# Ends of two softmax attention layers in a four-layer transformer kernel: channel order made by DMA during the layer, and results taken chunk by chunk

## The chip, the cores and the metric

The kernel runs on one core of one Trainium2 chip. The time is the device time of one execution in microseconds (us). The core has TensorE (PE; its weight loads are listed as PEld), VectorE (DVE), ScalarE (ACT), GpSimd (POOL), SyncE (SP), and 16 DMA engines. SP computes nothing here and issues most DMAs. Each engine runs its own instructions in order and waits for others on semaphores.

## The reference, cut to what matters

x has 2 batches of 1024 tokens of 128 channels in float32. Four layers follow one another, each an attention and a feed-forward part, each with a modulated layernorm in front and a gated residual. The change concerns the ends of the attention in layers 0 and 1:

```
# layer 0: two softmax maps per head, 16 heads of 8 channels
lam  = exp(sum(lambda_q1*lambda_k1)) - exp(sum(lambda_q2*lambda_k2)) + LAMBDA_INIT
attn = (map0 - lam * map1) @ v
attn = attn * rsqrt(mean(attn^2 over the 8 channels of a head) + 1e-5)
attn = attn * subln_w * (1 - LAMBDA_INIT)
x    = x + ga * (attn @ Wo.T)
# layer 1: plain softmax attention with a key mask, 16 heads
x    = x + ga * (softmax(q k^T / sqrt(8)) v @ Wo.T + bo)
# then, in both layers, layernorm of x and the feed-forward part
```

## The kernel before, in words

x stays in SBUF as [128 channels, 2, 1024]. NC = 4 chunks c of CW = 512 tokens cut it: chunk 0 and 1 are batch 0, chunk 2 and 3 batch 1. PSUM is one tensor `ps` of 8 banks of 512 columns.

**The softmax stage** (`softmax_stage`, used by layer 0 with the tile prefix a0 and by layer 1 with a1) works in units u, 32 in layer 0 and 16 in layer 1. Two groups of four maps make a pair kk (PAIRS is 8 and 4), and a pair has two halves of 512 queries, so n = 2*kk + half counts 16 halves in layer 0 and 8 in layer 1, with two units per half. In a unit PE makes scores in eight slots of keys (line 833), ACT takes their exponential (919), PE multiplies with the values (847) into bank 6, and meanwhile DVE finds the row maxima of the next unit (products 813, reduction 938), which POOL splits into bf16 parts (765 to 773). In the last unit there is no next one.

When a half is complete, ACT copies bank 6 to `o` (`take`, 899). Rows 32*j + 16*g + 0..7 of `o` hold 8 channels of map j of group g, row +8 its denominator. For every half but the last, SP then moves the denominators through DRAM into a packed tile (729, 731), ACT takes Ln and Exp there (904, 909; at slot 5 of the unit after the `take`), SP brings the reciprocals back through DRAM, broadcast over the rows (733, 735), and POOL divides (`divide`, 778) into `A.on`, which holds all halves. For the odd halves up to n = 11 SP then issues 36 loads of operands for later pairs (415), for the even ones from n = 2 to n = 12 it issues 12. SP takes up the next half only after them. The last half has no unit to hide behind: `take`, a product that spreads the denominators (`spread`, 856), Ln and Exp on ACT (929, 931), and a division on DVE (`divide_last`, 960).

**The end of layer 0** (`diff_out_stage`, line 1014) begins when all 16 halves are divided. Per chunk four products with `pick` (1031) accumulate map0 - lam*map1 in channel order; ACT squares (1059), DVE copies out scaled by the sub-norm weight (1068); `head_sum` (1036) adds the squares of a head, ACT takes Ln and Exp (1061, 1063), `head_spread` (1041) spreads the result over the channels, DVE multiplies (1072), PE multiplies with Wo (1044), DVE adds to x (1076). Each step runs over all four chunks before the next begins.

**The end of layer 1** (`out_stage` with the name o1 and two parts, line 1083) waits for all 8 halves, makes two products per chunk (1094), and DVE adds the bias (1123) and then the gated sum (1126).

Both ends interleave on PE the products of the following norm: `centre(c)` (302, bank 4 + c) once x of the chunk is there, `variance(c)` (307, bank c). The norm's ACT program squares (328), and takes Ln and Exp (332, 334), in the order square 0, square 1, invert 0, square 2, invert 1, square 3, invert 2, invert 3; DVE applies (314, 316). The norm's SP program (321) loads the weights of the next part; on SP it stands right behind the softmax stage's. A float32 product of 512 columns is two matmul instructions in the trace.

Of the kernel before, what the change touches and what calls it, by code (L numbers as in the profile page):

```python
# [15 lines left out]
F32 = mybir.dt.float32  # L16
# [619 lines left out]
def softmax_stage(nc, R, ctx, W, A):  # L636
# [26 lines left out]
    logged, inverted, divided, last_rec = (sem(n) for n in ("logged", "inverted", "divided", "last_rec"))  # L663
    den_dram, rec_dram = (nc.dram_tensor(pre + n, [2, 8, CW], F32, kind="Internal").ap() for n in ("den", "rec"))
# [49 lines left out]
    def on_sp(sp):  # L714
# [11 lines left out]
        for n in range(2 * PAIRS - 1):  # L726
# [14 lines left out]
            if n >= 2 and not c and kk - 1 < PAIRS:  # L741
                for operand in range(2):
                    load_rows(A, 2 * kk - 1, (kk - 1) % 2 * 2 + 1, operand, sp, heads=range(2, 4))

    def on_pool(pool):
# [38 lines left out]
        for u in range(UNITS - 1):  # L784
# [6 lines left out]
            if u and u % 2 == 0:  # L791
                divide(u // 2 - 1)

    def on_pe(pe):
# [94 lines left out]
        for half in range(2):  # L889
            pv(UNITS - 1, 7, half)  # L890
        spread()

    def on_act(act):
# [32 lines left out]
        take(PAIRS - 1, 1)  # L926
        act.wait_ge(bank_full, filled("spread"))
        act.wait_ge(divided, 2 * PAIRS - 2)
        act.activation(rec[:, 1, :], R.ps[:, dve_bank("spread"), :], ACT.Ln).then_inc(last_rec, 1)
        act.wait_ge(last_rec, 1)  # L930
        act.activation(rec[:, 1, :], rec[:, 1, :], ACT.Exp, scale=-1.0).then_inc(last_rec, 1)

    def on_dve(dve):
# [22 lines left out]
        def divide_last():  # L956

            dve.wait_ge(last_rec, 2)
            dve.wait_ge(divided, 2 * PAIRS - 1)
            dve.tensor_tensor(A.on[:, PAIRS - 1, CW:T], o[:, 1, :], rec[:, 1, :], ALU.mult).then_inc(divided, 1)  # L960
# [20 lines left out]
        divide_last()  # L981
# [32 lines left out]
def diff_out_stage(nc, R, ctx, W, A, join):  # L1014

    PAIRS = A.groups // 2 // B
# [3 lines left out]
    a, sq = R.xc, R.sq  # L1020
    dev = sb("dev", [128, 2, CW])
    got, copied, squared, ms, deviated, inverted, spread, normed, proj, done = (
        sem(n) for n in ("got", "copied", "squared", "ms", "dev", "inverted", "spread", "normed", "proj", "done"))
    A.finished, join.ready = (done, NC), [(done, c + 1) for c in range(NC)]

    def on_pe(pe):
        pe.wait_ge(*A.divided)
        for c in range(NC):
            b, t = chunk(c)
            for g in range(PAIRS):  # L1030
                last = pe.matmul(R.ps[:, c, :], pick[:, g, :], A.on[:, b * PAIRS + g, t], start=(g == 0),
                                 stop=(g == PAIRS - 1))
            last.then_inc(got, 1)
        for c in range(NC):
            pe.wait_ge(squared, c + 1)
            last = pe.matmul(R.ps[32 * c:32 * c + 32, 4, :], W.head_sum[:], sq[:, c, :], start=True, stop=True)
        last.then_inc(ms, 1)
        pe.wait_ge(inverted, 1)
        pe.wait_ge(copied, NC)
        for c in range(NC):  # L1040
            pe.matmul(R.ps[:, c, :], W.head_spread[:, c, :], dev[:, 1, :], start=True, stop=True).then_inc(spread, 1)
        for c in range(NC):
            pe.wait_ge(normed, c + 1)
            pe.matmul(R.ps[:, 4 + c, :], wo[:], a[:, c, :], start=True, stop=True).then_inc(proj, 1)
            if c == 2:
                join.norm.centre(pe, 0)
        join.norm.centre(pe, 1)
        join.norm.variance(pe, 0)
        join.norm.centre(pe, 2)
# [6 lines left out]
    def on_act(act):  # L1056
        for c in range(NC):
            act.wait_ge(got, c + 1)
            act.activation(sq[:, c, :], R.ps[:, c, :], ACT.Square, scale=8 ** -0.5).then_inc(squared, 1)
        act.wait_ge(ms, 1)  # L1060
        act.activation(dev[:, 0, :], R.ps[:, 4, :], ACT.Ln, bias=R.eps[:]).then_inc(deviated, 1)
        act.wait_ge(deviated, 1)
        act.activation(dev[:, 1, :], dev[:, 0, :], ACT.Exp, scale=-0.5).then_inc(inverted, 1)

    def on_dve(dve):
        for c in range(NC):
            dve.wait_ge(squared, c + 1)
            dve.tensor_scalar(a[:, c, :], R.ps[:, c, :], cols[:, 7:8], None, ALU.mult).then_inc(copied, 1)
        for c in range(NC):
            dve.wait_ge(copied, c + 1)  # L1070
            dve.wait_ge(spread, c + 1)
            dve.tensor_tensor(a[:, c, :], a[:, c, :], R.ps[:, c, :], ALU.mult).then_inc(normed, 1)
        for c in range(NC):
# [3 lines left out]
                                     ALU.mult, ALU.add).then_inc(done, 1)  # L1077
        join.norm.apply(dve, 0)
# [4 lines left out]
def out_stage(nc, R, ctx, W, layer, half, name, rhs, parts, w, ready, join, bias=None):  # L1083

    tmp = R.rstd
    proj, biased, done = (nc.alloc_semaphore(name + n) for n in ("proj", "biased", "done"))
    join.ready = [(done, c + 1) for c in range(NC)]

    def on_pe(pe):
        pe.wait_ge(W.loaded, W.count)  # L1090
        for c in range(NC):
            pe.wait_ge(*ready(c))
            for i in range(parts):
                last = pe.matmul(R.ps[:, c, :], w[:, i, :], rhs(i, c), start=(i == 0), stop=(i == parts - 1))  # L1094
                if parts > 2 and c == 3 and i == parts // 2:
# [3 lines left out]
            if c == 2 or c == 3 and parts <= 2:  # L1099
# [1344 lines left out]
```

## Time and profile before

| | us |
|---|---|
| median of 3 runs | 2280.16 |
| lowest and highest of them | 2278.03, 2281.89 |
| the profiled execution | 2285.85 |
| its span in the trace | 2284.1 |

The execution that was profiled took 2285.85 us; all rows are from it. Times in the trace count from the start of its span, and 1.75 us of the execution lie outside the span. The mean granted clock of TensorE over the span was 0.974 of full speed. The softmax stage of layer 0 ends near 684 us, that of layer 1 near 1124 us. Layers 2 and 3 follow and aren't touched but for two waits.

### The profile page before, as it was taken

The numbers are of one execution on the slowest core, as the hardware profiler recorded it, in microseconds if no ns is written. First come the engines' busy times: TensorE is split into PE (matmuls) and PEld (weight loads), VectorE is DVE, ScalarE is ACT, GpSimd is POOL, SyncE is SP. The second block draws the span as 40 slices with busy tenths as digits, with TensorE's granted clock in tenths as the row PEclk, the third lists the DMA queues.
The fourth block names the chain that finished last, engine by engine and source line by source line (L and its number), as shares of the span: only waits on it lengthen the run. The fifth ranks groups of instructions, "written<-read, shape, count | busy, mean of one in ns | idle before, by whom it ended". The sixth has DMA issues, their size and how long they took to land. (4 is left out here: it accounts for less than half of the span.)

```text
span 2284.1 us, 40826 instructions
## 1 busy us (share of the span) xinstructions
PE 2092.2 (92%) x15948; PEld 926.4 (41%) x15948; DVE 1597.6 (70%) x2012; ACT 1359.4 (60%) x2700; POOL 212.8 (9%) x393
## 2 busy tenths in 40 slices
PE   5899999999989689999989999999998989999999
PEld 3222222222224222222336666656666434444454
DVE  5999999999954699999365555555555265555553
ACT  3599999999983369999744444444444232222243
POOL 3011111010102501111000000000000010000000
PEclk7799999999999789999999999999999999999999
DMA  4000000000000200110100100011010125455520
GB/s 134 15 13 20 24 20 17 19 25 19 16 23 0 86 28 17 30 37 10 28 4 11 23 14 16 18 17 20 11 20 17 29 49 129 114 127 117 123 63 19
DMA packets 107966, 86.76 MB, mean 38 GB/s; under 512 B 50837, under 2 KB 91669, under 8 KB 103824
## 3 DMA queue, kind: packets, MB, share of 16 engines
q1 hardware_dynamic: 105780, 82.77, 14.7%
q8 instruction: 122, 2.00, 0.4%
q10 hardware_dynamic: 668, 1.04, 0.1%
q0 software_dynamic: 1344, 0.52, 0.1%
q14 instruction: 52, 0.43, 0.1%
HBM read 75.63 MB, written 8.73 MB: 37 GB/s over the span
## 5 line engine op out<-in xcount | busy, mean ns | idle before, releaser
L919 ACT ACTIVATE a0p<-ps 128x512 f32<-128x512 f32 x1024 | 544.3, 599 | 88.4 <-PE ps L833 71.8
L938 DVE TENSOR_REDUCE a0nm<-ps 128x2 f32<-128x1024 f32 x512 | 586.1, 1212 | 13.1 <-PE ps L813 10.9
L847 PE MATMUL ps<-a0p,a0vst 128*32 128x256 f32 x4096 | 328.6, 393 | 28.1 <-ACT a0p L919 14.6
L919 ACT ACTIVATE a1p<-ps 128x512 f32<-128x512 f32 x512 | 275.6, 596 | 57.2 <-PE ps L833 48.2
L938 DVE TENSOR_REDUCE a1nm<-ps 128x2 f32<-128x1024 f32 x256 | 294.2, 1213 | 11.5 <-PE ps L813 10.6
L833 PE MATMUL ps<-a0qm,a0k 32*128 32x512 bf16 x1024 | 276.8, 387 | 0.0
L1674 DVE TENSOR_REDUCE canm<-ps 128x1 f32<-128x128 f32 (+7 forms) x256 | 182.0, 752 | 115.3 <-PE ps L1537 114.6
L1625 ACT ACTIVATE cap_long<-ps,canm 128x1024 f32<-128x1024 f32 (+3 forms) x128 | 121.6, 953 | 190.1 <-DVE canm L1674 190.1
L813 PE MATMUL ps<-a0k,a0q 32*128 32x512 bf16 x1024 | 203.8, 396 | 29.4 <-DVE a0nm L938 21.7
L1906 ACT ACTIVATE ex_s<-ps 128x512 f32<-128x512 f32 x128 | 76.4, 597 | 252.9 <-PE ps L1861 252.9
L813 PE MATMUL ps<-a1k,a1q 64*128 64x512 bf16 x512 | 150.2, 404 | 27.0 <-DMA a1k<-a1mask 14.9
L847 PE MATMUL ps<-a1p,a1vst 128*32 128x256 f32 x2048 | 163.9, 392 | 7.0 <-ACT a1p L919 6.1
L1995 DVE TENSOR_TENSOR ex_su<-ex_s,ps 128x512 f32<-128x512 f32 x128 | 88.1, 688 | 116.9 <-PE ps L1865 115.7
L833 PEld LDWEIGHTS ps<-a0qm,a0k 32*128 32x128 bf16 x1024 | 79.1, 91 | 209.1 <-ACT a0p L919 119.8
L1537 PE MATMUL ps<-cak,caq 64*128 64x512 f32 (+3 forms) x768 | 158.6, 517 | 0.0
L833 PE MATMUL ps<-a1qm,a1k 64*128 64x512 bf16 x512 | 156.2, 385 | 0.0
L1550 PE MATMUL ps<-ident_res,cap_long 128*128 128x128 f32 x832 | 123.2, 281 | 29.1 <-ACT cap_long L1625 18.8
L847 PEld LDWEIGHTS ps<-a0p,a0vst 128*32 128x32 f32 x4096 | 81.5, 108 | 156.3 <-ACT a0p L919 71.0
L1865 PE MATMUL ps<-h_res,f2wu 128*128 128x512 f32 x256 | 130.7, 592 | 0.0
L1861 PE MATMUL ps<-h_res,f2wg 128*128 128x512 f32 x256 | 130.7, 592 | 0.0
L1849 PE MATMUL ps<-ex_hid,f2wd 128*128 128x512 f32 x256 | 130.5, 592 | 0.0
L1550 PEld LDWEIGHTS ps<-ident_res,cap_long 128*128 128x128 f32 x832 | 89.0, 140 | 86.0 <-issue 39.2
(300 smaller groups left out, 2535.5 us busy)
## 6 DMA issues: line engine op xcount, KB each, us to landing
ex_wb<-ex_w_dram SPq DMA_DIRECT2D x62, 512.0 KB, 6.2
carrow<-car_dram SPq DMA_DIRECT2D x32, 256.0 KB, 4.3
xc_res<-a0rec SPq DMA_DIRECT2D x15, 256.0 KB
a0parts<-a0parts_sb SPq DMA_DIRECT2D x8, 384.0 KB, 3.6
a1parts<-a1parts_sb SPq DMA_DIRECT2D x8, 384.0 KB, 3.5
f2wg<-in_ex_gate SPq DMA_DIRECT2D x32, 64.0 KB, 1.8
f2wu<-in_ex_up SPq DMA_DIRECT2D x32, 64.0 KB, 1.9
f2wd<-in_ex_down SPq DMA_DIRECT2D x32, 64.0 KB, 1.9
```

The lines of the kernel that those rows point to most:

```text
L813: pe.matmul(R.ps[:, bank + d, :], q[rows, slot, rt, t0:t0 + 128], k[rows, slot, rt, hf * CW:(hf + 1) * CW], start=True, stop=True).then_in ...
L833: pe.matmul(R.ps[:, score_bank(n), :], k[rows, place(u)[3], rt, s * 128:(s + 1) * 128], qm[rows, u % 2, rt, :], start=True, stop=True).the ...
L847: last = pe.matmul(R.ps[32 * j:32 * j + 32, 6, cols], vst[:, g, s, j * HG // 4, :], p[:, s % 2, j, cols], start=(g == 0 and s == 0 and hal ...
L919: act.activation(p[:, s % 2, e, :], R.ps[:, score_bank(n), :], ACT.Exp).then_inc(exp_done, 1)
L938: dve.tensor_reduce(nm[:, u % 2, tb, 2 - 2 * z:4 - 2 * z, hf], R.ps[:, bank:bank + 2, :], X_AXIS, ALU.max, negate=True).then_inc(bank_free, 1)
L1537: last = pe.matmul(R.ps[:, 2 * hh + c, 0:cols], q[rows, hp % 2, b, tb * 128:(tb + 1) * 128], k[rows, hp % 2, b, c * CW:c * CW + cols], sta ...
L1550: last = pe.transpose(R.ps[:, bank, to:to + 128], p[long][:, hh, s * 128:(s + 1) * 128], R.ident[:])
L1625: act.activation(p[long][:, hh, 0:(tb + 1) * 128], src, ACT.Exp, bias=nm[:, a % 4:a % 4 + 1], accum_out=rs[:, b, tb, hh:hh + 1]).then_inc( ...
L1674: dve.tensor_reduce(nm[:, a % 4:a % 4 + 1], src, X_AXIS, ALU.max, negate=True).then_inc(max_done, 1)
L1849: pe.matmul(R.ps[:, i % 4, :], wd[:, (i // 4) % 2, :], hid[:, i % 4, :], start=False, stop=True, skip_group_check=True).then_inc(d_done, 1)
L1861: pe.matmul(R.ps[:, G_BANK + 2 * (i % 2), :], wg[:, slot, :], h_chunk(R, c), start=True, stop=True)\
L1865: pe.matmul(R.ps[:, U_BANK + 2 * (i % 2), :], wu[:, slot, :], h_chunk(R, c), start=True, stop=True)\
```

## The change

In layer 0:

- After each of the first 15 halves is divided, SP issues eight DMAs of 8 rows by 512 columns. They move the rows of `A.on` into `A.maps`, in channel order, one tile for map 0 and one for map 1. `A.on` now holds two halves in turn. SP waits for the division first, and these DMAs stand on SP behind the operand loads of that half. POOL waits, before it divides half n, for the DMAs of half n - 2.
- At the end of its softmax program, DVE forms map0 - lam*map1 by one instruction per chunk (128 rows, for chunk 3 the 96 rows that don't come from the last half), into `rstd`, in the order 0, 1, 3, 2. POOL squares each.
- On PE three `head_sum` products (chunks 0 to 2) stand ahead of the last two value products of the last unit (`last_products`); on ACT their Ln and Exp stand ahead of the last `take`. `head_spread` for chunk 0 stands ahead of the `spread` product, those of chunks 1 and 2 and the Wo product of chunk 0 behind it. Between these DVE does the sub-norm multiply (one instruction for weight and norm), the last division, and the addition to x.
- The last half passes one `pick` product with 32 output rows, then square, `head_sum`, Ln, Exp and `head_spread` for chunk 3 on 32 rows.

In layer 1 `value_out_stage` takes the place of `out_stage`: the product of chunk 0 stands ahead of `last_products`, that of chunk 1 behind `spread`, that of chunk 2 waits for 7 halves, that of chunk 3 for 8. The bias times the gate is added to x by DVE before the first result. Cut to its core:

```diff
@@ on_sp, for each half n but the last, behind the operand loads
+            if A.maps:
+                b, pair = n // 2 // (PAIRS // B), n // 2 % (PAIRS // B)
+                sp.wait_ge(divided, n + 1)
+                for g in range(2):
+                    for j in range(4):
+                        r, ch = 32 * j + 16 * g, 32 * pair + 16 * g + 8 * (j // 2)
+                        sp.dma_start(A.maps[ch:ch + 8, j % 2, b, c * CW:c * CW + CW], A.on[r:r + 8, c, :]).then_inc(gathered[c], 16)
@@ on_pool
         def divide(n):
             pool.wait_ge(rec_in[n % 2], 16 * (n // 2 + 1))
+            if A.maps and n >= 2:
+                pool.wait_ge(gathered[n % 2], 128 * (n // 2))
...
+        if A.maps:
+            for i, (c, rows) in enumerate(COMBINED):
+                pool.wait_ge(combined, i + 1)
+                pool.tensor_tensor(R.sq[rows, c, :], R.rstd[rows, c, :], R.rstd[rows, c, :], ALU.mult).then_inc(map_squared, 1)
@@ on_dve of the softmax stage
-        divide_last()
+        if A.maps:
+            for c, rows in COMBINED:
+                b, t = chunk(c)
+                halves = (b + 1) * (PAIRS // B) - (c == 3)
+                dve.wait_ge(gathered[c % 2], 128 * halves)
+                dve.scalar_tensor_tensor(R.rstd[rows, c, :], A.maps[rows, 1, b, t], W.cols[rows, 4:5], A.maps[rows, 0, b, t],
+                                         ALU.mult, ALU.add).then_inc(combined, 1)
@@ diff_out_stage, on_pe
-        pe.wait_ge(*A.divided)
-        for c in range(NC):
-            b, t = chunk(c)
-            for g in range(PAIRS):
-                last = pe.matmul(R.ps[:, c, :], pick[:, g, :], A.on[:, b * PAIRS + g, t], start=(g == 0),
...
+        pe.wait_ge(A.map_squared, 4)
+        for c in range(3):
+            last = pe.matmul(R.ps[32 * c:32 * c + 32, MS[0], :], W.head_sum[:], sq[:, c, :], start=True, stop=True)
+        last.then_inc(ms, 1)
+        A.last_products()
+        pe.wait_ge(inverted, 1)
+        head_spread(0)
+        A.last_spread()
+        head_spread(1)
+        head_spread(2)
+        output(0)
+        pe.wait_ge(*A.divided)
+        pe.matmul(R.ps[late, PICKED, :], pick[:, 3, late], A.on[:, 1, :], start=True, stop=True).then_inc(picked, 1)
+        output(1)
+        pe.wait_ge(squared, 1)
+        pe.matmul(R.ps[late, MS[1], :], W.head_sum[:], sq[:, 3, :], start=True, stop=True).then_inc(ms, 1)
+        output(2)
+        join.norm.centre(pe, 0)
+        pe.wait_ge(copied, 1)
+        pe.wait_ge(inverted, 2)
+        head_spread(3)
         join.norm.centre(pe, 1)
         join.norm.variance(pe, 0)
+        output(3)
@@ diff_out_stage, on_act
+        invert(0, early)
+        A.last_take()
+        A.last_reciprocal()
+        act.wait_ge(picked, 1)
+        act.activation(sq[late, 3, :], R.ps[late, PICKED, :], ACT.Square).then_inc(squared, 1)
+        invert(1, late)
@@ diff_out_stage, on_dve
+        norm(0)
+        norm(1)
+        A.last_divide()
+        norm(2)
+        result(0)
+        dve.wait_ge(squared, 1)
+        dve.tensor_copy(a[late, 3, :], R.ps[late, PICKED, :]).then_inc(copied, 1)
+        result(1)
+        result(2)
+        dve.wait_ge(copied, 1)
+        norm(3)
+        result(3)
         join.norm.apply(dve, 0)
@@ value_out_stage (new, layer 1), on_pe
+        output(0)
+        A.last_products()
+        A.last_spread()
+        output(1)
+        output(2)
+        join.norm.centre(pe, 0)
+        output(3)
+        join.norm.variance(pe, 0)
+        join.norm.centre(pe, 1)
+        join.norm.centre(pe, 2)
+        join.norm.variance(pe, 1)
+        join.norm.centre(pe, 3)
+        join.norm.variance(pe, 2)
+        join.norm.variance(pe, 3)
@@ value_out_stage, on_dve
+        dve.tensor_scalar(lift[:], R.gate[:, 2 * B:3 * B], W.bo[:], None, ALU.mult).then_inc(lifted, 1)
+        dve.wait_ge(lifted, 1)
+        for b in range(B):
+            dve.tensor_scalar(R.x[:, b], R.x[:, b], lift[:, b:b + 1], None, ALU.add).then_inc(lifted, 1)
+        result(0)
+        A.last_divide()
+        for c in range(1, NC):
+            result(c)
+        join.norm.apply(dve, 0)
```

## Rows read from the trace of the kernel before

**Rows 1.** The page: busy us of each engine (share of the span), instructions.
```profile
PE 2092.2 (92%) x15948; PEld 926.4 (41%) x15948; DVE 1597.6 (70%) x2012; ACT 1359.4 (60%) x2700; POOL 212.8 (9%) x393
```

**Rows 2.** Timeline, end of layer 0: start us, us, engine, line, out<-in, count [idle before <-releaser].
```profile
679.28 1.07 PE L847 MATMUL ps<-a0p,a0vst 128*32 128x256 f32 x16 [0.60 <-ACT a0p L919]
680.42 0.60 ACT L899 ACTIVATE a0o<-ps 128x512 f32<-128x512 f32 x1 [1.19 <-PE ps L847]
682.25 0.60 ACT L929 ACTIVATE xc_res<-ps 128x512 f32<-128x512 f32 x1 [1.23 <-PE ps L856]
683.54 0.69 DVE L960 TENSOR_TENSOR a0on<-a0o,xc_res 128x512 f32<-128x512 f32 x1 [23.38 <-ACT xc_res L931]
684.29 15.68 PE L1031 MATMUL ps<-a0on,a0pick 128*128 128x512 f32 x32 [2.08 <-DVE a0on L960]
701.74 0.69 ACT L1061 ACTIVATE do_dev<-ps,eps_res 128x512 f32<-128x512 f32 x1 [1.14 <-PE ps L1036]
706.67 2.74 PE L1044 MATMUL ps<-xc_res,a0wo 128*128 128x512 f32 x6
711.17 0.75 DVE L1076 SCALAR_TENSOR_TENSOR x_res<-ps,gate_res,x_res 128x512 f32<-128x512 f32 x1 [0.96 <-PE ps L1044]
714.40 1.02 PE L302 MATMUL ps<-x_res,centre_res 128*128 128x512 f32 x2
714.62 0.68 ACT L332 ACTIVATE rstd_res<-ps,eps_res 128x512 f32<-128x512 f32 x1
```

**Rows 3.** Windows (busy us of each engine, clock, DMA share, GB/s) at the ends.
```profile
683.00:684.00 1.00, 0.00 (x0) 0.00 (x0) 0.46 (x1) 0.51 (x1) 0.00 (x0) 1.00 0.00 0
685.00:686.00 1.00, 1.00 (x2) 0.34 (x1) 0.00 (x0) 0.00 (x0) 0.00 (x0) 0.50 0.00 0
688.00:689.00 1.00, 1.00 (x3) 0.38 (x2) 0.00 (x0) 0.00 (x0) 0.00 (x0) 1.00 0.00 0
1145.00:1150.00 5.00, 3.23 (x6) 0.78 (x6) 4.78 (x9) 2.00 (x4) 0.00 (x0) 1.00 0.01 3
```

**Rows 4.** Timeline of POOL and SP late in layer 0, the same columns.
```profile
662.70 1.27 POOL L778 TENSOR_TENSOR a0on<-a0o,xc_res 128x512 f32<-128x512 f32 x1 [4.74 <-DMA xc_res<-a0rec]
646.42 0.58 SPq L729 DMA_DIRECT2D a0den<-a0o  x1
648.19 0.32 SPq L731 DMA_DIRECT2D a0packed<-a0den  x1
659.89 1.31 SPq L321 DMA_DIRECT2D f0w<-in_L_fW2T  x1
666.96 0.43 SPq L321 DMA_DIRECT2D decay_res<-in_L_norm  x1
```

**Rows 5.** Timeline of SP and ACT around the tightest and an ordinary odd half.
```profile
264.07 3.67 SPq L415 DMA_DIRECT2D a0k<-a0parts  x6
268.23 0.62 SPq L729 DMA_DIRECT2D a0den<-a0o  x1
277.67 0.24 ACT L904 ACTIVATE a0packed<-a0packed 128x32 f32<-128x32 f32 x1
413.29 3.67 SPq L415 DMA_DIRECT2D a0k<-a0parts  x6
428.94 0.24 ACT L904 ACTIVATE a0packed<-a0packed 128x32 f32<-128x32 f32 x1
```

**Rows 6.** Timeline, end of layer 1, and the bias of layer 0's feed-forward part.
```profile
733.85 3.10 DVE L1267 TENSOR_SCALAR x_res<-x_res,ff0lift 128x1024 f32<-128x1024 f32 x2
1120.57 0.60 ACT L899 ACTIVATE a1o<-ps 128x512 f32<-128x512 f32 x1 [1.19 <-PE ps L847]
1124.53 7.08 PE L1094 MATMUL ps<-a1on,a1wo 128*128 128x512 f32 x12 [2.17 <-DVE a1on L960]
1135.08 0.60 ACT L328 ACTIVATE sq_res<-ps 128x512 f32<-128x512 f32 x1 [1.98 <-PE ps L302]
1137.32 0.69 DVE L314 TENSOR_TENSOR xc_res<-rstd_res,ps 128x512 f32<-128x512 f32 x1 [1.56 <-ACT rstd_res L334]
```

More of the change, by code:

```diff
@@ L888, in on_pe, with last_products @@
                     turn(u + 1)
-        for half in range(2):
-            pv(UNITS - 1, 7, half)
-        spread()
+        def last_products():
+            for half in range(2):
+                pv(UNITS - 1, 7, half)
+        A.last_products, A.last_spread = last_products, spread
     def on_act(act):
@@ L925, in on_act, with last_reciprocal @@
                         invert(u // 2 - 1)
[L926 to L931, printed above, removed]
+        def last_reciprocal():
+            act.wait_ge(bank_full, filled("spread"))
+            act.wait_ge(divided, 2 * PAIRS - 2)
+            act.activation(rec[:, 1, :], R.ps[:, dve_bank("spread"), :], ACT.Ln).then_inc(last_rec, 1)
+            act.wait_ge(last_rec, 1)
+            act.activation(rec[:, 1, :], rec[:, 1, :], ACT.Exp, scale=-1.0).then_inc(last_rec, 1)
+        A.last_take, A.last_reciprocal = lambda: take(PAIRS - 1, 1), last_reciprocal
     def on_dve(dve):
@@ L1034, in on_pe, with head_spread @@
[L1034 to L1042, printed above, removed]
+        def head_spread(c):
+            rows = late if c == 3 else early
+            pe.matmul(R.ps[:, SPREAD[c], :], W.head_spread[rows, c, :], dev[rows, 1, :], start=True, stop=True).then_inc(spread, 1)
@@ L1056, in on_act, with invert, norm, result @@
     def on_act(act):
[L1057 to L1063, printed above, removed]
-    def on_dve(dve):
[L1066 to L1070, printed above, removed]
+        def invert(i, rows):
+            act.wait_ge(ms, i + 1)
+            act.activation(dev[rows, 0, :], R.ps[rows, MS[i], :], ACT.Ln, bias=R.eps[rows], scale=0.125).then_inc(deviated, 1)
+            act.wait_ge(deviated, i + 1)
+            act.activation(dev[rows, 1, :], dev[rows, 0, :], ACT.Exp, scale=-0.5).then_inc(inverted, 1)
+        invert(0, early)
[4 more added lines that the diff above has]
+        invert(1, late)
+    def on_dve(dve):
+        def norm(c):
             dve.wait_ge(spread, c + 1)
-            dve.tensor_tensor(a[:, c, :], a[:, c, :], R.ps[:, c, :], ALU.mult).then_inc(normed, 1)
-        for c in range(NC):
+            dve.scalar_tensor_tensor(a[:, c, :], a[:, c, :], cols[:, 7:8], R.ps[:, SPREAD[c], :], ALU.mult, ALU.mult)\
+               .then_inc(normed, 1)
+        def result(c):
             b, t = chunk(c)
@@ L1087, in out_stage @@
+def out_stage(nc, R, ctx, W, layer, half, name, rhs, parts, w, ready, join):
+    proj, done = (nc.alloc_semaphore(name + n) for n in ("proj", "done"))
     join.ready = [(done, c + 1) for c in range(NC)]
@@ L1098, in on_pe @@
             last.then_inc(proj, 1)
-            if c == 2 or c == 3 and parts <= 2:
-                join.norm.centre(pe, c - 2)
-            if c == 3 and parts <= 2:
-                join.norm.variance(pe, 0)
-        if parts <= 2:
-            join.norm.centre(pe, 2)
-            join.norm.variance(pe, 1)
-            join.norm.centre(pe, 3)
-        else:
-            join.norm.variance(pe, 1)
-            join.norm.centre(pe, 2)
-            join.norm.centre(pe, 3)
+            if c == 2:
+                join.norm.centre(pe, 0)
+        join.norm.variance(pe, 1)
+        join.norm.centre(pe, 2)
+        join.norm.centre(pe, 3)
         join.norm.variance(pe, 2)
@@ L1115, in on_dve @@
     def on_dve(dve):
-        dve.wait_ge(W.loaded, W.count)
         for c in range(NC):
```

77 lines of the change are left out of this document (49 added, 28 removed).

## The prediction

> **What bounds the kernel now.** I read the page first: PE is busy for 92% of the span [rows 1], but a busy share doesn't say what a stage's end costs, so I went to the timeline of the two ends. In layer 0 the last exponentials are followed by a chain in which each engine waits for another: value products, `take`, spread, Ln, Exp, division, and only then, at 684.29, the 32 `pick` instructions, 15.68 us long [rows 2]. The windows show that PE, which had only the `spread` product between 680.4 and 684.3, then works at half clock (0.50, that is 1.2 GHz) and is back at full (2.4 GHz) by 688 [rows 3]. After `pick` comes the second chain, Ln, Exp, `head_spread`, multiply, Wo, to the last addition at 711.17 and `centre(3)` at 714.40 [rows 2]. Only half 15 needs the first chain: half 14 was divided at 662.70, and neither DVE nor POOL has other work afterwards [rows 4]; DVE's 23.38 us of idle time before line 960 say the same [rows 2]. Layer 1 ends likewise, with 7.08 us for the first 12 product instructions [rows 6]. So the bound is latency on one chain, not an engine, and what is taken off that chain comes off the time.
>
> **Prices.** A float32 product of 512 columns costs PE 0.86 us: six instructions of Wo took 2.74, one lasts 0.59, so the pitch is (2.74 - 0.59)/5 = 0.43 and a product has two. From issue to its reader's start it is 1.23 - 0.1 = about 1.1 us [rows 2]. On ACT Copy or Square costs 0.60, Ln 0.69, Exp 0.63, on DVE 0.69 to 0.75, on POOL 1.27 [rows 2, 4].
>
> **Layer 0, covered work.** Half 14 is divided at 664.0. SP then issues eight DMAs. The trace has no SBUF to SBUF copy; its nearest row is the store of the denominators, also 8 rows of 2 KB: 0.58 to 0.62 to issue, and the next DMA, which waits for it, starts 1.77 after it [rows 4, 5]. Bounds: 0.32 (the packed load) to 1.31 (the largest load) each [rows 4]; I take 0.6. Eight end at 668.8 and the last lands near 670. DVE combines (0.75), POOL squares (1.27): 672.2. The squares of chunks 0, 1 and 3 (3 x 1.27 from 664.0) are done at 667.8. PE needs all four at about 678.6, so 6 us are spare; the cover is the last unit, and without it the chain of 8 us would be paid in full. The weight loads of the next part (line 321), which began right after the broadcast of half 14 and ended by 667.4 [rows 4], move back by up to 9 us, to 677; the feed-forward part uses them after 690.
>
> **Layer 0, mid-stage.** The eight DMAs also stand behind the 36 operand loads of the six odd halves up to 11. Ordinarily those end at 413.29 + 3.67 = 416.96, and ACT takes the Ln of the next half at 428.94; in the tightest case they end at 267.74 and Ln starts at 277.67 [rows 5]. The store of the denominators, the packed load and its landing take about 1.8 + 2.0 = 3.8 us (the 2.0 is an estimate from the 1.77 of the same-sized store). That leaves 8.2 and 6.1 us for eight issues, 1.02 and 0.77 us each; at 0.6 nothing stalls (zero cost, cover 1.3 us in the worst half). POOL's new wait for the DMAs of half n - 2 and the queue of loads for later pairs have tens of us.
>
> **Layer 0, the new tail**, with PE at full clock. PE is free at 678.6, three `head_sum` deliver at 679.7. ACT: Ln, Exp to 681.1, then `take` to 681.7 (0.7 later than before: the price of putting them ahead of it). `head_spread(0)` fills PE to 682.0, `spread` reaches ACT at 683.1, Ln and Exp end at 684.4. Meanwhile `head_spread` 1 and 2 and Wo(0) run to 685.4. DVE divides after its second multiply, to 685.4; `pick` reaches ACT at 686.6, Square (687.2), `head_sum` (688.4), Ln and Exp (689.7). PE fills in with Wo(1), Wo(2) and `centre(0)`. Then four products in PE's order, `head_spread(3)`, `centre(1)`, `variance(0)`, Wo(3), end at 693.2; DVE's last addition starts at 693.4; `centre(2)`, `variance(1)` follow and `centre(3)` starts at 694.9 instead of 714.40. The norm's second Ln starts at 695.0 instead of 714.62 [rows 2]. Gain **19.5 us**.
>
> **Layer 1.** Wo(0), two products or 1.72 us, starts when PE is free at 1118.7 and delays the last value products: `take` starts 1.0 later than 1120.57. `spread` leaves PE at 1123.1, chunks 1 and 2 take until 1126.5 while ACT and DVE finish the last half (1125.4), `centre(0)` to 1127.4, chunk 3 to 1129.1, `variance(0)`, and `centre(1)` to 1130.8. ACT's Square of chunk 1 starts at 1131.0 instead of 1135.08, and from there ACT works without gaps; the first apply on DVE starts at 1133.0 instead of 1137.32 [rows 6]. The bias additions (3.10 us on DVE, by the two in layer 0 [rows 6]) lie in its idle last unit. Gain **4.3 us**. Bounds for this term: 3 (apply pushed behind the results on DVE) to 6 (the start of `variance(0)` moves by 5.8).
>
> **Sum.** 19.5 + 4.3 = 23.8 us, so 2285.85 - 23.8 = 2262.0 for the profiled execution. That one took 5.7 us more than the median; the median of the runs comes to 2280.16 - 23.8 = **2256.4**.
>
> **A rule that speaks against it.** The store of 16 KB took 0.6 us to issue and 1.77 to complete, and six loads are issued in 3.67 us without waiting for one another [rows 4, 5]. The Trainium skill, page DMA: Bandwidth & Descriptors, section Rules for kernel authors, says that transfers under 64 KB pay mostly overhead and should be joined; its section Latency and other measured facts names about 2 us of fixed cost. If eight DMAs paid that one after another, an estimate by that page would be 16 us a half. By the rows the overhead overlaps; the rule's outcome is the second rival, priced from rows there.
>
> **Rival 1: the clock falls in the new tails.** Before, it fell after 4 us in which PE was nearly idle and came back after 3.5 us of full work; at 65% busy (3.23 of 5.00) it stayed at 2.4 GHz [rows 3]. In the new tails I count PE busy for over 80% between 681 and 688 and for about 70% between 1121 and 1124.5, which speaks for a full clock. Against: many short waits. At half clock a product costs 0.86 more. On the path stand twelve in layer 0 (some 8 uncovered, 7 us) and ten in layer 1 (some 6, 5 us): 2256.4 + 12 = **2268.4**. The skill's page TensorE: Matmul & The Clock Gate, section HAM oscillation — how this bites in real kernels, tells of short bursts of products between waits that each begin cold; it would choose this rival. Chance 0.15.
>
> **Rival 2: slower, through SP's queue.** SP is in order, and behind the eight DMAs waits the next half's store of denominators, for which ACT stalls amid the exponentials of slot 5; PE and everything else wait for ACT. With d us for each DMA, five halves lose 8d - 8.2 and one 8d - 6.1. At d = 1.31 that is 5 x 2.3 + 4.4 = 16, and the gain shrinks to 8. It decides from 48d - 47.1 = 23.8, d = 1.48. At d = 2 (each issued only when the one before is done, as 1.77 suggests [rows 4]), the loss is 49 us; moreover the last half lands at about 681 and PE waits some 5 us: 2256.4 + 49 + 5 = **2310**. For it: the one completion that the trace shows. Against: 36 loads in a row at 0.61 each [rows 5]. Chance 0.04.
>
> **Rival 3: part of it is lost to stalls.** DMAs at 1.0 to 1.31, or POOL and DVE late, so that PE waits at 678.6, or the feed-forward weights late: **2266**. Chance 0.06.
>
> **Rival 4: more comes back.** The full clock keeps a second stretch alive in the norm or the feed-forward part, and layer 1 gives 6: **2252**. Chance 0.07. That the change doesn't do what it says is hard to see, since all its instructions are plain in the diff; a cost I haven't seen that takes back the gain within 0.2% or beyond: 0.03.
>
> **How the numbers follow.** The forecast has 0.65. The range reaches from Rival 4, less 1 us of scatter between runs, to Rival 1 with the same: 2251 to 2269.5. It holds the forecast, Rival 4, most of Rival 1 and of Rival 3. Left out are Rival 2, the unseen cost and the outer parts of the others. A measurement of this kernel can tell about 0.2%, 4.6 us, from no change. Faster by more: the forecast, Rivals 1, 3 and 4, 0.93; within it 0.03; slower 0.04, Rival 2 and a little of the unseen.
>
> **What would show each step.** Line 1031's 32 instructions are gone, and two with 32 output rows stand after the last division. The gather DMAs last about 0.6 us on SP, the last eight end near 669, and the Ln of each later half starts in ACT's rhythm, 37.8 us after the one before, without a gap. POOL's four squares end before 673 and PE doesn't wait between the last scores and `head_sum`. `take` starts near 681.1 and 1121.6, the granted clock stays 1.00 from 681 to 696 and from 1121 to 1134, and `centre(3)` starts near 695 in layer 0. A clock of 0.50 in either tail speaks for Rival 1, gaps before ACT's Ln in slot 5 for Rival 2. The prediction is wrong if the span between the last exponential and the norm's first apply shrinks by less than 15 us in layer 0, or if the attention stage itself gets longer.

## The result, and the profile after

The change took the median from 2280.26 us (4 runs) to **2264.11 us** (4 runs, 2262.16 to 2265.14), a ratio of 0.9929 [0.9912, 0.9946]: 16.1 us gained where 23.8 were forecast. The profiled execution took 2265.14 us, the longest of the four. The page after, to be held against [rows 1]:

```profile
span 2263.4 us, 40899 instructions
PE 2077.2 (92%) x15918; PEld 918.9 (41%) x15918; DVE 1595.7 (71%) x2012; ACT 1358.9 (60%) x2699; POOL 216.5 (10%) x397
```

PE's busy time fell by 15.0 us, about what `pick` took (15.68 us [rows 2]); its share is what it was. The new end of layer 0 in the timeline of after, beside [rows 2] (columns: start, length, engine, line, operation, tiles, shape, count, and the idle time before it with its releaser):

```profile
676.26 1.03 PE L1078 MATMUL ps<-sq_res,a0head_sum 128*32 128x512 f32 x6
677.35 0.68 ACT L1110 ACTIVATE do_dev<-ps,eps_res 96x512 f32<-96x512 f32 x1 [0.36 <-PE ps L1078]
678.60 0.57 ACT L924 ACTIVATE a0o<-ps 128x512 f32<-128x512 f32 x1
683.24 1.04 PE L1088 MATMUL ps<-a0on,a0pick 128*32 128x512 f32 x2
684.32 0.59 ACT L1118 ACTIVATE sq_res<-ps 32x512 f32<-32x512 f32 x1 [2.30 <-PE ps L1088]
686.25 1.13 PE L1074 MATMUL ps<-rstd_res,a0wo 128*128 128x512 f32 x2
686.36 0.68 ACT L1110 ACTIVATE do_dev<-ps,eps_res 32x512 f32<-32x512 f32 x1 [1.44 <-PE ps L1091]
687.07 0.63 ACT L1112 ACTIVATE do_dev<-do_dev 32x512 f32<-32x512 f32 x1
687.21 1.02 PE L302 MATMUL ps<-x_res,centre_res 128*128 128x512 f32 x2
688.16 1.12 PE L1070 MATMUL ps<-do_dev,a0head_spread 32*128 32x512 f32 x2
692.09 0.75 DVE L1130 SCALAR_TENSOR_TENSOR x_res<-ps,gate_res,x_res 128x512 f32<-128x512 f32 x1 [1.96 <-PE ps L1074]
693.61 1.02 PE L302 MATMUL ps<-x_res,centre_res 128*128 128x512 f32 x2
693.81 0.69 ACT L332 ACTIVATE rstd_res<-ps,eps_res 128x512 f32<-128x512 f32 x1 [0.26 <-PE ps L307]
```

This execution ran 2.24 us ahead of that of before already at half 14's `take` (643.56 against 645.80), so 2.24 is added when its times are compared with the prediction's. The clock of the new tail, by windows (length, then busy time and count of PE, PEld, DVE, ACT, POOL, then the granted clock, DMA share, GB/s):

```profile
681.00:683.00 2.00, 2.00 (x6) 0.76 (x4) 1.37 (x3) 0.99 (x2) 0.00 (x0) 1.00 0.00 0
695.00:697.00 2.00, 1.83 (x7) 0.39 (x4) 1.15 (x3) 1.97 (x5) 0.00 (x0) 1.00 0.00 0
...
700.00:702.00 2.00, 2.00 (x4) 0.84 (x4) 0.55 (x1) 0.00 (x0) 0.00 (x0) 0.50 0.00 0
702.00:704.00 2.00, 2.00 (x4) 0.83 (x3) 0.00 (x0) 0.69 (x1) 0.00 (x0) 0.50 0.00 0
```

It is full through the tail and falls only behind it, in the feed-forward part. SP, DVE and POOL, the covered work, beside [rows 4]:

```profile
661.38 5.31 SPq L761 DMA_DIRECT2D a0maps<-a0on  x8
668.06 0.75 DVE L1016 SCALAR_TENSOR_TENSOR rstd_res<-a0maps,a0cols 128x512 f32<-128x512 f32 x1 [8.16 <-DMA a0maps<-a0on]
668.89 1.04 POOL L815 TENSOR_TENSOR sq_res<-rstd_res 128x512 f32<-128x512 f32 x1 [4.54 <-DVE rstd_res L1016]
```

The end of layer 1, beside [rows 6]. Up to half 6's `take` this execution was 17.58 us ahead of that of before (1067.79 against 1085.37):

```profile
1101.18 1.98 PE L1164 MATMUL ps<-a1on,a1wo 128*128 128x512 f32 x4
1104.23 0.60 ACT L924 ACTIVATE a1o<-ps 128x512 f32<-128x512 f32 x1 [2.43 <-PE ps L870]
1113.78 0.60 ACT L328 ACTIVATE sq_res<-ps 128x512 f32<-128x512 f32 x1 [2.84 <-PE ps L302]
1115.65 0.69 DVE L314 TENSOR_TENSOR xc_res<-rstd_res,ps 128x512 f32<-128x512 f32 x1 [2.83 <-ACT rstd_res L334]
```

A part of both gains is the clock. Before ran at 0.50 for 3.4 us in each end (684.3 to 687.7 in `pick`, 1124.6 to 1128.0 in the Wo products of layer 1), each time after some 4 us in which PE had only the `spread` product; after has no such stretch in either end. At the full-clock pitch of 0.43 the 32 instructions of `pick` would have taken 13.9 us instead of 15.68, and the 12 of layer 1 5.3 instead of 7.08, an estimate of 1.8 us each. One window of layer 1's end from before, then one from after:

```profile
1126.00:1128.00 2.00, 2.00 (x3) 0.66 (x2) 0.00 (x0) 0.00 (x0) 0.00 (x0) 0.50 0.00 0
```

```profile
1105.00:1107.00 2.00, 2.00 (x5) 0.95 (x6) 0.00 (x0) 0.91 (x2) 0.00 (x0) 1.00 0.00 0
```

**The span cut into stretches** says where the gain went. Each number below is the distance of two rows of one timeline, in us. Borders: half 14's `take`; the last Ln of the norm behind layer 0; the last Ln of the norm behind the feed-forward part; half 6's `take` in layer 1; the last Ln of the norm behind layer 1; the first product of layer 2's attention; the last product of the experts; the end. The other columns are experiments, told below.

| stretch | before | b0 | dma | l1 | l0 | after | a1 | pad_control | pad_before | pad_l0 | v2 | pad_order |
|---|---|---|---|---|---|---|---|---|---|---|---|---|
| start | 645.8 | 646.1 | 644.9 | 644.5 | 645.0 | 643.6 | 645.5 | 645.9 | 646.5 | 643.4 | 644.7 | 644.0 |
| end of layer 0 | 71.86 | 71.88 | 71.85 | 71.82 | 53.30 | 53.30 | 53.31 | 53.31 | 71.79 | 53.32 | 53.31 | 53.31 |
| feed-forward | 43.47 | 43.47 | 43.47 | 43.47 | 45.94 | 45.79 | 46.08 | 46.16 | 41.19 | 41.38 | 41.39 | 41.38 |
| layer 1's halves | 324.2 | 324.3 | 324.3 | 324.2 | 323.6 | 325.1 | 325.3 | 325.2 | 325.3 | 324.4 | 324.6 | 325.6 |
| end of layer 1 | 55.35 | 55.35 | 55.36 | 51.26 | 55.12 | 51.26 | 51.26 | 51.26 | 55.34 | 55.19 | 51.26 | 50.45 |
| into layer 2 | 41.38 | 41.42 | 41.43 | 41.50 | 41.45 | 42.95 | 42.94 | 42.90 | 42.70 | 41.45 | 41.45 | 42.97 |
| layer 2 | 1015.6 | 1014.9 | 1015.3 | 1013.9 | 1015.1 | 1015.3 | 1013.8 | 1015.6 | 1015.0 | 1015.5 | 1015.4 | 1015.5 |
| layer 3's end | 86.4 | 83.5 | 83.2 | 88.7 | 86.1 | 86.1 | 88.7 | 86.1 | 81.3 | 83.8 | 83.8 | 83.9 |

Between before and after the two ends gain 18.56 + 4.09 = 22.65. Behind them 2.3 (feed-forward), 0.9 (layer 1's halves) and 1.6 (into layer 2) are given back, and layer 3's end, 86.1 here, is dearer than the 83.5 and 83.2 of the two other kernels whose code there is that of before (b0 and dma). The profiled executions differ by 20.7 us, more than the medians' 16.1: the one of after was already 2.24 us ahead at the table's first row, and that of before had a long end of layer 3. The first row lies between 643.4 and 645.9 in kernels with the new layer 0 and between 644.5 and 646.5 in those with the old, so nothing shows that the change earns those 2.24.

### The profile page after: what moved, and what is told of

Read it like the earlier page. It is cut to its first block and busy times, and to the rows that moved or that the text cites. A ratio compares the mean times of both kernels' runs of the same rounds, so it can differ in the third digit from the quotient of the medians.

```text
span 2263.4 us, 40899 instructions
## 1 busy us (share of the span) xinstructions
PE 2077.2 (92%) x15918; PEld 918.9 (41%) x15918; DVE 1595.7 (71%) x2012; ACT 1358.9 (60%) x2699; POOL 216.5 (10%) x397
## 3 DMA queue, kind: packets, MB, share of 16 engines
q1 hardware_dynamic: 107700, 84.74, 15.4%
q10 hardware_dynamic: 668, 1.04, 0.1%
```

## The experiments

Four kernels ran together first, beside 27 runs of before (2280.97). **b0** is the kernel before, unchanged.

> The kernel before, unchanged, profiled once more on this chip. Theory A (the two tails gave what the trace shows, and the rest of the shortfall is time that other stages and the profiled execution itself gain or lose with TensorE's clock): its profile lies nearer to its median, some 3 to 5 us below 2285.85, with its first take near 114 instead of 116.3 us, or other stretches at half clock shorter. Theory B (the change costs something between the tails, by its DMAs): this profile is again near 2285 us and the stretches at half clock are the same as in the first.

It took 2281.38 (2280.05 to 2282.67, 11 runs), ratio 1.0003 [0.9994, 1.0012], and its profiled execution 2282.66. So the profiled execution on which the prediction's sum was made (2285.85) was a long one: its layer 3's end was 2.9 us longer than b0's. The start was not the reason: b0's first `take` came at 116.56, before's at 116.32, and not near 114 as the expectation's Theory A had it.

**l0** is after with the softmax program and the out stage of layer 1 put back; **l1** is after with layer 0's put back.

```diff
 # l0; l1 has `not A.mask` and the old diff_out_stage
+        if A.mask:
+            last_products()
+            spread()
...
-            stages += [value_out_stage(nc, R, ctx, WA1, A1, after_a1)]
+            stages += [old_out_stage(nc, R, ctx, WA1, 1, 0, "o1", lambda i, c: A1.on[:, (c // 2) * 2 + i, chunk(c)[1]], 2, WA1.wo,
+                                     lambda c: A1.divided, after_a1, WA1.bo)]
```

> Only layer 0 is changed; layer 1 has its old end. Theory A: layer 0's tail alone is worth 18.5 us, less 1 to 3 us that the following feed-forward part loses to a longer stretch at half clock: 2262 to 2266 us against 2280. Theory B: the loss lies in layer 0's stage, so this part gives no more than 13 us, 2267 us or above.

> Only layer 1 is changed; layer 0 has its old end and no gather DMAs. Theory A: 4 us, so 2276 us, within 1.5 us of scatter. Theory B says the same of this part. A third possibility, that layer 1's part is worth nothing because the following stage takes it back, gives 2280.

l0 took 2268.30 (2265.21 to 2271.87), ratio 0.9948 [0.9935, 0.9962]; l1 2281.20 (2276.67 to 2283.55), ratio 0.9999 [0.9990, 1.0008]. The two ends do in each what they do together (18.6 in l0, 4.1 in l1, by the table). But layer 1's 4.1 us don't reach the end of the program: in l1's profile layer 3's end is 88.7 instead of b0's 83.5. And the 12.7 of l0 with the 0 of l1 is less than the 16.1 of both together. l0 took a time that the expectation had given to Theory B (a loss in layer 0's stage), which its 53.30 us for that stage contradict; l1 lies next to the expectation's third possibility, but the time is not taken back in the stage that follows: "into layer 2" is 41.50 there and 41.38 before.

**What I had overlooked** explains a good part of both. The diff also edits `out_stage`, which layers 2 and 3 keep using; the cut of the diff shown ahead of the prediction leaves that out, the sentence there that layers 2 and 3 aren't touched but for two waits is wrong, and the prediction doesn't price it. With layer 1 gone from it, its branch for few parts was removed:

```diff
-                if parts > 2 and c == 3 and i == parts // 2:
+                if c == 3 and i == parts // 2:
                     join.norm.variance(pe, 0)
                     join.norm.centre(pe, 1)
...
-            if parts > 2 and c == 2:
+            if c == 2:
                 join.norm.apply(dve, 0)
-        if parts <= 2:
-            join.norm.apply(dve, 0)
```

Layer 3 has one part, and so it changed to the order of layer 2, in which DVE applies the norm of chunk 0 ahead of the last addition. All kernels made from after carry it, l0 and l1 among them, so their two gains together pay for it twice: about 2.5 of the 3.4 us that the two parts are short of the whole. Its price is read where the clock is 1.00 throughout, from the timelines of pad_before (old order) and v2 (new order); these kernels are told below. pad_before, DVE and the first product of the feed-forward part:

```profile
2231.83 2.40 DVE L1126 SCALAR_TENSOR_TENSOR x_res<-ps,gate_res,x_res 128x512 f32<-128x512 f32 x3 [0.17 <-PE ps L1094]
2235.20 0.75 DVE L1126 SCALAR_TENSOR_TENSOR x_res<-ps,gate_res,x_res 128x512 f32<-128x512 f32 x1 [0.97 <-PE ps L1094]
2240.14 0.38 PE L1160 MATMUL ps<-ident_res,h_res 128*8 128x128 f32 x2
```

The same in v2, and PE's product that waits:

```profile
2205.98 2.47 DVE L1237 SCALAR_TENSOR_TENSOR x_res<-ps,gate_res,x_res 128x512 f32<-128x512 f32 x3
2213.10 0.69 DVE L314 TENSOR_TENSOR xc_res<-rstd_res,ps 128x512 f32<-128x512 f32 x1 [4.64 <-ACT rstd_res L334]
2214.28 0.74 DVE L1237 SCALAR_TENSOR_TENSOR x_res<-ps,gate_res,x_res 128x512 f32<-128x512 f32 x1
2215.08 1.12 PE L302 MATMUL ps<-x_res,centre_res 128*128 128x512 f32 x2 [1.22 <-DVE x_res L1237]
2216.90 0.38 PE L1269 MATMUL ps<-ident_res,h_res 128*8 128x128 f32 x2
```

From the first addition to the last it takes 8.30 us instead of 3.37, because DVE stands 4.64 us in front of the apply, for ACT, and `centre(3)` then waits for DVE. The feed-forward part starts 10.92 us after the first addition instead of 8.31: 2.6 us, and the stretch's 83.8 against 81.3 says 2.5. In l1 that is about half of its 5.2 us; the clock is the rest. In the kernels with unpadded products the clock comes on top, and two prices fit all twelve columns: 81.3 with the old order or 83.8 with the new one; 1.9 to 2.3 more where the windows show one stretch of 0.50, 3.4 us long (b0, dma; l0, after, pad_control); 4.9 to 5.1 more where they show one of 6.8 and one of 3.4 (before; l1, a1). Two windows of l1, one from each of its stretches there, and one of dma from the later part, where b0 and dma have none:

```profile
2242.00:2244.00 2.00, 2.00 (x3) 0.67 (x2) 0.00 (x0) 0.69 (x1) 0.00 (x0) 0.50 0.00 0
2254.00:2256.00 2.00, 2.00 (x3) 0.67 (x2) 1.64 (x3) 0.00 (x0) 0.00 (x0) 0.50 0.00 0
```

```profile
2259.00:2261.00 2.00, 2.00 (x6) 0.87 (x5) 0.75 (x1) 0.85 (x2) 0.00 (x0) 1.00 0.13 48
```

All windows of dma from 2255 to 2263 show 1.00. A kernel with the rest of the change and the old order in layer 3 would show it directly; it was not tried.

**dma** is before with the change's 120 gather DMAs, whose result nobody reads (DVE waits for them at the end of the stage); nothing else of the change is in it.

```diff
+            if A.maps:
+                b, pair = n // 2 // (PAIRS // B), n // 2 % (PAIRS // B)
+                sp.wait_ge(divided, n + 1)
+                if n >= 8:
+                    sp.wait_ge(gathered[c], 128 * (n // 2))
+                for g in range(2):
+                    for j in range(4):
+                        r, ch = 32 * j + 16 * g, 32 * pair + 16 * g + 8 * (j // 2)
+                        sp.dma_start(A.maps[ch:ch + 8, j % 2, c * CW:c * CW + CW], A.on[r:r + 8, n // 2, c * CW:c * CW + CW]).then_inc(gathered[c], 16)
```

> The kernel before, with the 120 gather DMAs added to SP's queue and their results unused; it computes all that it did. Theory A: no stall, the takes of layer 0 stay 37.82 us apart, time 2280 us within 1 us. Theory B (SP's queue delays the denominators, or the DMAs disturb others): 2283 to 2288 us, with takes further apart in the six intervals behind odd halves.

2281.63 (2279.61 to 2284.63, 11 runs), ratio 1.0004 [0.9995, 1.0013]. SP's timeline:

```profile
662.65 5.31 SPq L754 DMA_DIRECT2D a0maps<-a0on  x8
668.00 0.44 SPq L321 DMA_DIRECT2D f0w<-in_L_fW1T  x1
```

Eight take 5.31 us, 0.66 each, and ACT's takes stay at their 37.8 us distance (380.1 to 455.8 for three, as the view of that line has it):

```profile
L910 ACT ACTIVATE a0o<-ps x3: 597/597/598, 380.1 to 455.8; 128x512 f32<-128x512 f32 x3
```

The gathers cost nothing that shows: the interval of the ratio leaves room for 3 us, but a stall of ACT would part the takes, and they stay 37.82 us apart up to half 14 in dma and in after alike. So the second rival, and the queue's share of the third, are out.

**a1** is after again, unchanged, and **l1p1** and **l1p3** are l1 with one and three extra products (0.86 us each) ahead of chunk 2's own, which overwrite their result. They were to tell whether l1's lost gain depends on where in time the later stages lie. With **v2** they ran beside 23 runs of before (2280.76).

> The changed kernel, unchanged, with more runs and one more profile. Both theories: 2264 us within 1 us. Theory A (the profile shows the half-clock stretches where the first one had them, since the program starts in step with the clock's changes): three stretches' worth of half clock in the feed-forward part of layer 0 (6.8 and 3.4 us long) and one early in layer 2. Theory C (which stretches come is left to chance): others than those, and a spread between runs that explains the loss without any rule.

> The kernel with layer 1 alone changed (2281.2 us), with one float32 product more ahead of chunk 2's in layer 1's end: 0.86 us of work on the chain, its result overwritten. Theory A (where later stretches at half clock fall depends on how far the work before them is shifted): the time differs from 2281.2 + 0.86 by a microsecond or more, most likely below it. Theory C (chance, the same for each kernel): 2282.1 us.

```diff
             pe.wait_ge(A.divided[0], 2 * PARTS * (b + 1) - 1 + c % 2)
+            for _ in range(1 if c == 2 else 0):
+                pe.matmul(R.ps[:, BANK[c], :], W.wo[:, 0, :], A.on[:, b * PARTS, t], start=True, stop=True)
```

> The same with three products more, 2.6 us on the chain, all overwritten. Theory A: not 2283.8; at 2280 to 2282 more work costs nothing, since layer 3's end gets back what its two extra half-clock stretches took. Theory C: 2283.8 us.

a1: 2264.49 (2258.77 to 2268.65, 6 runs), ratio 0.9922 [0.9910, 0.9934]. l1p1: 2280.80 (2279.03 to 2286.55), ratio 1.0001 [0.9992, 1.0010]; l1p3: 2284.16 (2281.55 to 2285.85), ratio 1.0013 [1.0004, 1.0021]. The tail grew by just what was added (52.12 and 53.83 instead of 51.26), and three products cost the program 3.0 us for 2.6, one product -0.4 for 0.86. The medians decide little, and Theory A's 2280 to 2282 for three products did not come: 2284.16 is next to Theory C's 2283.8. a1 speaks for neither theory alone: in layer 0's feed-forward part and on the way into layer 2 its profile has the stretches of half clock that after's has, in layer 3's end it has two (6.8 and 3.4 us, 88.7) where after's has one (3.4 us, 86.1), and its six runs spread over 9.9 us. The profile of l1p1 shows why one profile can't decide either: its layer 0, whose code is l1's, took 73.22 instead of 71.82 and its feed-forward part 45.96 instead of 43.47. In both profiles the way into layer 2 took 1.3 us longer (42.77 and 42.87) than l1's 41.50, with a stretch of half clock there that l1 doesn't have.

**v2** goes at the clock itself. In after it falls at 698.8, while PE runs the small products of the feed-forward part, whose operands have 8 rows. v2 is after with these operands on 128 rows, of which 120 are zero, so that the result is the same.

```diff
-    pairs = sb("pairs", [8, B, 2, C])
-    bd = sb("bd", [8, B, 8, C])
+    pairs = sb("pairs", [128, B, 2, C])
+    bd = sb("bd", [128, B, 8, C])
...
+    def on_pool(pool):
+        pool.wait_ge(*rows.ready[NC - 1])
+        pool.memset(pairs[:], 0.0).then_inc(turned, 1)
+        pool.memset(bd[:], 0.0).then_inc(turned, 1)
```

> The changed kernel, with the operands of the small products in both feed-forward parts with LoRA (8 rows) padded with zeros to 128 rows: the same products in the same number of columns, and results unchanged. Theory A with the reason that products of 8 rows let the clock fall: the clock stays at 1.00 in the feed-forward part of layer 0 and near 2240 us, and the time falls by 4 to 8 us, to 2256 to 2260. If the rows don't matter (the gaps between the products do): the stretches stay and the time is 2264, or 1 us more for the memsets.

v2 took **2258.37** (2257.40 to 2259.91, 4 runs), ratio 0.9902 [0.9887, 0.9916]. Its control **pad_control** has the tiles, the memsets and the wait of v2, but its products read 8 rows; **pad_before** is before with the padding, **pad_l0** is l0 with it, and **pad_order** is v2 with two moves in the PE program of `value_out_stage`. They ran beside 17 runs of before (2281.39).

```diff
 # pad_control against v2 (one of its three places)
-            pe.matmul(R.ps[:, 4 + 2 * b, :], odd, bd[:, b, 0:4, :], start=True, stop=True).then_inc(outer, 1)
+            pe.matmul(R.ps[:, 4 + 2 * b, :], odd, bd[0:8, b, 0:4, :], start=True, stop=True).then_inc(outer, 1)
 # pad_order against v2
-        output(0)
         A.last_products()
+        output(0)
         A.last_spread()
...
         join.norm.centre(pe, 0)
+        join.norm.centre(pe, 1)
         output(3)
         join.norm.variance(pe, 0)
-        join.norm.centre(pe, 1)
```

> The same kernel as v2 with its memsets, waits and tiles, but the small products read 8 rows again. If the rows of the products keep the clock up: the half-clock stretches are back and the time is 2264 to 2265. If it was the memsets or their timing: 2258.4.

2265.39 (2261.83 to 2268.31, 6 runs), ratio 0.9923 [0.9910, 0.9936]: 7.0 us above v2 by the number of rows alone. Its runs lie in two groups, three near 2262.4 and three near 2268.2, so the 7.0 is rough; but each of them is above each of v2's, and against before of its own set the difference is 6.4. The same products in the timelines of pad_control and of v2:

```profile
700.84 2.04 PE L1280 MATMUL ps<-ff0bd,ff0pairs 8*128 8x128 f32 x8 [0.17 <-DVE xc_res L314]
702.81 6.46 PE L1291 MATMUL ps<-h_res,ff0w1e 128*128 128x512 f32 x8
```

```profile
699.65 2.03 PE L1280 MATMUL ps<-ff0bd,ff0pairs 128*128 128x128 f32 x8 [0.17 <-DVE xc_res L314]
701.51 3.61 PE L1291 MATMUL ps<-h_res,ff0w1e 128*128 128x512 f32 x8
```

The small products take the same time either way; the eight behind them take 6.46 or 3.61. The windows, pad_control first, then v2:

```profile
702.00:704.00 2.00, 2.00 (x6) 1.23 (x6) 1.07 (x2) 0.00 (x0) 0.00 (x0) 0.50 0.00 0
```

```profile
702.00:704.00 2.00, 2.00 (x6) 0.90 (x5) 0.00 (x0) 1.25 (x2) 0.00 (x0) 1.00 0.00 0
```

The other profiles say the same. In all ten with 8 rows (before, b0, dma, l1, l1p1, l1p3, l0, after, a1, pad_control) the clock falls in both feed-forward parts with small products, 1.8 to 4.2 us after the first of them; in the four with 128 rows it falls in neither. Where it fell 1.8 to 2.6 us after the first, it stayed at 0.50 for 6.8 us and fell once more, for 3.4, at the second group of small products; where it fell 2.7 to 4.2 us after, one stretch of 3.4 us was all. In layer 0 the first happened in l0, after, a1 and pad_control, and in one of the six with the old end (l1p1). That is the 2.3 us that the feed-forward part gives back.

> The kernel before, with the small products of the two LoRA parts padded to 128 rows. It is the base for v2: with those stretches at half clock gone, the change alone remains between them. Theory A (the tails give 19.4 and 4.1 us, and the feed-forward parts took the rest back): 2276 to 2279 us, so that v2 (2258.4) lies 18 to 21 us below it, more than the 16.3 without padding. Theory C (the loss is elsewhere): v2 lies 16 us below it, so 2274.5.

2279.12 (2276.24 to 2280.90, 11 runs), ratio 0.9987 [0.9978, 0.9996]. Padding is worth 2.3 us on before and some 6 on after. With it in both, the change is worth 2279.12 - 2258.37 = **20.7 us**, where it is 16.1 without; the two kernels ran in different sets, and with each held against before of its own set it is 20.1. By the table the two ends gain 18.48 + 4.08 = 22.6 and the order in layer 3 costs 2.5: 20.1.

> The padded kernel with layer 0 alone changed, layer 1's end as before. Theory A: layer 1's part is worth 3 to 4 us once the later clock is steady: 2261.5 to 2262.5. Theory C (layer 1's part is worth nothing, as 2281.2 against 2281.0 says): 2258.4.

2261.80 (2260.33 to 2262.86, 5 runs), ratio 0.9911 [0.9898, 0.9924]. Both it and v2 have the new order in layer 3, and so between them stands layer 1's end alone: 3.4 us of the medians (2.8 against before of their own sets) for the 3.9 of its stretch. The gain that l1 seemed to lose is there once the rest is equal.

> The padded kernel v2, with two orders changed on TensorE in layer 1's end: chunk 0's product behind the last value products instead of ahead of them, and centre of chunk 1 ahead of chunk 3's product. By the trace the take comes 1.2 us earlier, and the Square of chunk 1 some 2 us after that of chunk 0 instead of 3.4: 2 us together, 2256 to 2257, unless half-clock stretches come back in the shorter tail (then 2258 to 2260).

2258.32 (2257.99 to 2258.88, 4 runs), ratio 0.9895 [0.9880, 0.9909], the same as v2. Its `take` is 1.24 us earlier again (35.20 after half 6's, as before, where v2 has 36.44), but the norm's first Ln waits for the `variance(0)` that stands behind the four product instructions of chunk 3, and the tail gains only 0.8 (50.45). Then a stretch of half clock comes back on the way into layer 2 and takes 1.5. PE's timeline and the windows there, of v2 and then of pad_order:

```profile
1141.58 1.12 PE L1484 MATMUL ps<-h_res,a2down 128*128 128x512 f32 x2 [0.17 <-DVE h_res L316]
1145.06 3.87 PE L1625 MATMUL ps<-h_res,a2qkv 128*128 128x512 f32 x8 [2.35 <-PEq L2468]
1143.00:1145.00 2.00, 0.00 (x0) 0.00 (x0) 0.00 (x0) 0.34 (x1) 0.00 (x0) 1.00 0.00 0
1145.00:1147.00 2.00, 1.94 (x5) 0.74 (x5) 0.69 (x1) 0.00 (x0) 0.00 (x0) 1.00 0.03 8
```

```profile
1141.06 1.12 PE L1484 MATMUL ps<-h_res,a2down 128*128 128x512 f32 x2 [0.17 <-DVE h_res L316]
1144.53 5.37 PE L1625 MATMUL ps<-h_res,a2qkv 128*128 128x512 f32 x8 [2.35 <-PEq L2468]
1143.00:1145.00 2.00, 0.47 (x1) 0.30 (x2) 0.00 (x0) 0.00 (x0) 0.00 (x0) 1.00 0.00 0
1145.00:1147.00 2.00, 2.00 (x4) 0.81 (x3) 0.69 (x1) 0.00 (x0) 0.00 (x0) 0.56 0.04 8
```

PE stands still for the same 2.35 us in both, half a us earlier in pad_order; v2 keeps 1.00 and pad_order falls, 0.7 us after the pause. All fourteen profiles have this pause, 2.29 to 2.35 us long. In seven the clock falls near its end, from 0.3 us before it to 1.2 after (after, a1, pad_control, pad_before, pad_order, l1p1, l1p3), in seven it doesn't (before, b0, dma, l1, l0, pad_l0, v2). Nothing that these runs vary explains which.

## Why the prediction was right or wrong

**Layer 0, covered work: right.** The gathers took 0.66 us each (I took 0.6) and, with the 2.24 added, the last eight ended at 668.9 (668.8), POOL's last square at 672.2 (672.2), and PE didn't wait: `head_sum` at 678.5 (678.6). POOL's square of one tile took 1.04, not the 1.27 of its product of two tiles that the working used.

**Layer 0, mid-stage: right.** Nothing stalled, by the dma kernel (ratio 1.0004) and by after's own takes, 37.82 us apart.

**Layer 0, the new tail: right but for 0.9 us.** `take` at 680.84 (681.1), `pick` at ACT at 686.56 (686.6), the second Ln at 688.60 (688.4). Then `head_spread(3)` starts at 690.40 where the working has 689.8, 0.46 us behind the end of the Exp that it waits for. For most of that PE was at `centre(0)`: its first instruction starts at 687.21, and at the pitch of 0.43 a third could follow at 688.07. The term that is off is the pitch. From `pick` to `head_spread(3)`, where waits stand between the products, one starts 0.95 to 1.05 us after the other, and I had 0.86. The products behind lose 0.3 more in the same way, and `centre(3)` is at 695.85 instead of 694.9, 18.55 earlier than before and not 19.5.

**Layer 1: right.** With the 17.58 added, `take` is at 1121.81 (1121.6), the Square of chunk 1 at 1131.36 (1131.0) and the first apply at 1133.23 (1133.0): 4.1 us where 4.3 were forecast.

**The sum: this step failed**, though 2264.1 lies inside the range. It carried 23.8 us from the ends to the end of the program as if all behind them stayed as it was. Two things there did not:
- The order of layer 3's end. I never priced the edit of `out_stage`: 2.5 us at full clock.
- The clock behind the tails. In the profiles 2.3 us in the feed-forward part, 0.9 in layer 1's halves and 1.6 into layer 2. Rival 1 looked for the fall in the tails, where it isn't; its 12 us were too many and its place wrong, but half clock is what takes the rest. Only the 2.3 us come with the change in the runs; the stretches in layer 1's halves and into layer 2 also come in pad_before, which lacks the change, and are missing in v2, which has it, so that these 2.5 us are not shown to be its price. That the padding is worth 6 on after and 2.3 on before puts some 4 us on the small products' clock in medians.

So 23.8 - 0.9 - 0.2 - 2.5 - 4.8 = 15.4 by the profiles' stretches, where the medians say 16.1. That the range held is in part luck: it was wide for a fall of the clock in the tails, which did not come, and neither the order of layer 3 nor a fall of the clock behind the tails is priced in a rival. The time is near Rival 3's 2266, but none of its stalls showed.

**Rivals.** Rival 1 did not come: after's clock is 1.00 in every window from 681 to 697 and from 1103 to 1115. The Trainium skill, page TensorE: Matmul & The Clock Gate, section HAM oscillation — how this bites in real kernels, tells of bursts that are shorter than the DMA waits between them and that each begin cold. The prediction had it choose Rival 1, and that was a misreading: in after's tails PE was idle for at most 0.76 us at a time, so they are not the page's case and don't test it. The Trainium skill, page DMA: Bandwidth & Descriptors, section Rules for kernel authors, says that transfers under 64 KB pay mostly overhead; whatever the overhead was, it had a cover here: 120 of 16 KB cost 0.66 us of SP's time each and nothing of the program's that shows. Rival 4, more than forecast, did not come.

**Left open:** what places a stretch of half clock in one execution and not in the next of the same code (l1p1 in layer 0; b0 and before in layer 3's end), and why seven of fourteen profiles have one on the way into layer 2, after the same pause, and seven none.

## What to carry to other kernels

Read the whole diff for shared functions, and price each other caller: a helper that lost one of its users also lost a branch that another still needed. Price a latency that is taken off between two stages with the stages behind it, above all where the profile before shows stretches at half clock there, and split a change only into parts that don't share an edit, else their gains don't add. The fastest kernels here are v2 and pad_order, 2258.4 and 2258.3: 22 to 23 us below before and 6 below the change.

## What was not expected of the hardware

The number of operand rows of a few short products decides the clock behind them. The eight small products take 2.04 us with 8 rows and 2.03 with 128; but with 8 (pad_control) the granted clock falls to 0.50 from 701.6 on, for 6.8 us and then again for 3.4, and with 128 (v2) it stays at 1.00 there. In the medians that is 7.0 us. And the same pause of PE, 2.29 to 2.35 us on the way into layer 2, was followed or met by a fall in seven profiles and passed at 1.00 in seven, v2 among them.
